# A two-layer graph network kernel: the edge phase cut into three parts, with one softmax over all edges and V and the receiver rows kept in DRAM

## The reference

```python
# layer 0: attention over the edges that end in a node, 8 heads of 32
qkv = x @ W_qkv.T + b_qkv
att = einsum('mhd,mhd->mh', Q[dst], K[src]) / sqrt(32)
e = exp(att - segment_max(att, dst)[dst])
attention = e / segment_sum(e, dst)[dst]
x = layernorm(x + segment_sum(attention * V[src], dst) @ W_ff.T + b_ff)
# layer 1: messages from the type of the sender, filtered by the edge
W = (edge_attr @ W_dist + b_dist) * cut(edge_weight)
agg = segment_sum(embed_table[node_type][src] * W, dst)
x = layernorm(x + concat([x, agg]) @ W_comb + b_comb)
```

## Time and profile before

| | before |
|---|---|
| three runs | 1411.08, 1412.26, 1413.56 us |
| median | 1412.26 us |
| span of the profiled execution | 1409.4 us |
| busy: PE, DVE, ACT, POOL | 85%, 85%, 63%, 76% |
| mean granted clock of PE | 0.972 |
| moved by DMA | 160.55 MB, 114 GB/s over the span |

### The profile page before, as it was taken

One profiled execution on the slowest core, in us unless ns is written; L12 is line 12 of the kernel. 1 busy time (PEld: TensorE's weight loads), 2 busy tenths in 40 slices (PEclk: granted clock), 3 DMA queues, 4 the chain that ended last, 5 costly groups with the idle time before them and its releaser, 6 DMA issues.

```text
span 1409.4 us, 30737 instructions
## 1 busy us (share of the span) xinstructions
PE 1197.9 (85%) x7469; PEld 1051.0 (75%) x7469; DVE 1193.5 (85%) x3044; ACT 891.5 (63%) x2560; POOL 1064.4 (76%) x1141
## 2 busy tenths in 40 slices
PE   2999999999999958888888888888888888888882
PEld 1788888888888857777777777777778777877872
DVE  3899999999999968888888888888888888888882
ACT  1788898988889954555555555555555555555541
POOL 1787878788888845877777777777877777777763
PEclk9999999999999989999999999999999999999996
DMA  5666666666666431111222221222222222222200
GB/s 165 231 228 216 229 215 228 216 225 220 228 219 227 174 118 42 52 55 56 58 59 60 61 61 58 61 61 62 62 62 62 62 62 58 62 62 62 61 29 27
DMA packets 76848, 160.55 MB, mean 114 GB/s; under 512 B 27159, under 2 KB 42514, under 8 KB 76758
## 3 DMA queue, kind: packets, MB, share of 16 engines
q1 hardware_dynamic: 59574, 124.18, 26.8%
q0 software_dynamic: 17248, 36.08, 8.5%
HBM read 98.65 MB, written 67.45 MB: 118 GB/s over the span
## 4 chain that ended last, share of the span: by engine, by line
POOL 39%; issue 34%; DVE 14%; ACT 4%; POOLq 3%; DMA 2%; PE 2%; SPq 1%; DVEq 1%; ACTq 0%
POOL zin L605 16%; POOL xd L659 6%; POOL xs L658 6%; POOL ub L667 3%; DVE den L1427 2%; DVE est L1335 2%; DVE t L1330 2%; DVE resc L1419 2%; DVE xs_lo L1325 2%; POOL ty_idx L612 2%; DVE xd_lo L1322 2%; POOL tyf L622 1%; ACT raw L1081 1%; POOL idx_b L648 1%; POOL ty L616 1%
## 5 line engine op out<-in xcount | busy, mean ns | idle before, releaser
L773 PE MATMUL ps<-w_mix,zT 128*128 128x256 f32 x1564 | 363.0, 385 | 19.6 <-ACT zT L957 18.4
L773 PEld LDWEIGHTS ps<-w_mix,zT 128*128 128x128 f32 x1564 | 290.4, 191 | 72.8 <-ACT zT L957 30.7
L605 POOL TENSOR_TENSOR zin<-xin,bff_row 128x1024 f32<-128x1024 f32 x98 | 231.9, 2367 | 2.2
L1266 DVE SCALAR_TENSOR_TENSOR yn<-ps,r,bc 128x256 f32<-128x256 f32 x391 | 162.2, 478 | 17.4 <-issue 12.2
L973 ACT ACTIVATE junk<-yn 128x256 f32<-128x256 f32 x391 | 156.9, 402 | 8.6 <-DVE yn L1266 8.4
L616 POOL DMA_INDIRECT ty<-in_node_type_dram,ty_idx x98 | 97.7, 997 | 84.3 <-DMA ty<-in_node_type_dram,ty_idx 50.4
L658 POOL DMA_INDIRECT xs<-in_x_dram,idx_b x98 | 116.7, 1191 | 52.9 <-issue 52.9
L1038 ACT ACTIVATE rdx<-rd 128x512 f32<-128x512 f32 x49 | 30.9, 631 | 197.2 <-DVE rd L1351 197.2
L699 POOL DMA_INDIRECT out_dram<-oe,idx_b x98 | 104.5, 1066 | 66.9 <-POOL idx_b L691 45.8
L1235 DVE BATCH_NORM_STATS2 stat<-zin 128x6 f32<-128x256 f32 x391 | 136.2, 407 | 4.6 <-POOL zin L605 4.6
L807 PE MATMUL ps<-xs_hi,w_hi 128*128 128x256 f32 x392 | 118.8, 303 | 11.1 <-DVE ye L1365 7.9
(11 more groups left out here) (173 smaller groups left out, 3675.7 us busy)
## 6 DMA issues: line engine op xcount, KB each, us to landing
xin<-in_x_dram SPq DMA_DIRECT2D x97, 512.0 KB, 3.7
out_dram<-on SPq DMA_DIRECT2D x97, 512.0 KB, 2.9
tybc<-type_rows SPq DMA_DIRECT2D x49, 128.0 KB, 3.4
dwin<-dst_o SPq DMA_DIRECT2D x47, 128.5 KB, 3.2
attr_o<-in_edge_attr_dram SPq DMA_DIRECT2D x1, 3125.0 KB, 13.5
at<-attr_o SPq DMA_DIRECT2D x48, 64.0 KB, 3.0
ty<-in_node_type_dram,ty_idx POOLq DMA_INDIRECT x98, 4.1
xs<-in_x_dram,idx_b POOLq DMA_INDIRECT x98, 3.4
```

Source lines behind the costliest of these rows:

```text
L605: pool.tensor_tensor(z, xx, bb, ALU.add).then_inc(n_z, 1)
L773: last = mm(ps[0:np_, 4 + 2 * (q % 2) + j // 2, (j % 2) * D:(j % 2 + 1) * D], zT[:, q % 2, k, j * P:j * P + np_], w_mix[:, k, :], start=k ...
L1266: last = dve.scalar_tensor_tensor(out=yn[0:np_, q, j * D:(j + 1) * D], in0=ps[0:np_, 4 + 2 * (q % 2) + j // 2, (j % 2) * D:(j % 2 + 1) * D ...
```

## The change

The edge phase becomes three parts, written out for all 49 blocks (no loops).

1. For every block: gathers, transposes, parts, Q, K and V. Q and K now have the edges in the partitions; their bias is added by a product of ones with the bias row. DVE multiplies them and a `tensor_reduce` over 32 channels gives the scores `att`. V and the transposed receiver rows are stored in DRAM (`v_o`, `xd_o`, 256 KB each a block).
2. The scores are transposed to 14 chunks x 8 heads = 112 partitions of 896 edges. Maximum, exponential, sum and division are done at once on [112, 896] tiles: scans inside a chunk in both directions, and short scans on one row for what crosses from chunk to chunk. The result, e / sum, goes to DRAM (`a_o`).
3. For every block SP loads back the receiver rows, V, the flags of equal receivers and the attention weights, broadcast over each head's 32 channels by four transfers. POOL multiplies weight and V, DVE scans the sums, and the rest follows as before (the roots now on ACT and DVE, the bias of the aggregate in the product, its copy on ACT).

The removed code is the old `edge` of every engine (the functions above). The core of what is added:

```diff
+        def keep(b):
+            par = b % 2
+            sp.wait_ge(e_xdc, b + 1)
+            sp.dma_start(xd_o[b], flat(xdT[:, par])).then_inc(e_xdo[par], 16)
+            if b:
+                sp.wait_ge(e_v, 2 * b)
+                sp.dma_start(v_o[b - 1], flat(vT[:, 1 - par])).then_inc(e_vo[1 - par], 16)
...
+        def static_loads(n):
+            par, h = n % 2, n // 2
+            after(sp, e_hot, n - 1)
+            sp.dma_start(tybc[:, par, :], type_blocks[n:n + 1, :].to_broadcast([P, EB])).then_inc(e_tb[par], 16)
+            after(sp, e_atc, 3 * (n - 1))
...
+                sp.dma_start(at[:, par, :, :], attr_blocks[n]).then_inc(e_at[par], 16)
+            after(sp, e_z, 2 * (n - 1))
+            sp.dma_start(flat(xd2[:, par]), xd_o[n]).then_inc(l_x[par], 16)
+            after(sp, e_ev, n - 1)
+            sp.dma_start(flat(v2[:, par]), v_o[n]).then_inc(l_ev[par], 16)
+            after(sp, e_agg, 2 * (n - 1))
+            sp.dma_start(sbc[:, par, :], row(same_o, EB * n, EB * (n + 1)).to_broadcast([P, EB])).then_inc(l_s[par], 16)
+
+        def attention_load(n):
+            par = n % 2
+            after(sp, e_ev, n - 1)
+            for q in range(HPC):
+                sp.dma_start(abc[q * HD:(q + 1) * HD, par],
+                             a_o[q:H8:HPC, EB * n:EB * (n + 1)].rearrange("(a c) n -> a c n", a=1).to_broadcast([HD, DC, EB])).then_inc(l_ev[par], 16)
...
+        for n in range(2):
+            static_loads(n)
+        sp.wait_ge(c_step, step["attention"])
+        sp.dma_start(a_o.rearrange("h (t j) -> t h j", t=NCH), a_c[:]).then_inc(c_out, 16)
+        sp.wait_ge(c_out, 16)
+        for n in range(2):
+            attention_load(n)
+        for n in range(2, B):
+            static_loads(n)
+            attention_load(n)
```

```diff
+        def weigh(n):
+            par, h = n % 2, n // 2
+            pool.wait_ge(l_ev[par], 80 * (h + 1))
+            after(pool, e_num, 2 * (n - 1))
+            pool.tensor_tensor(ev[:, par], abc[:, par], v2[:, par], ALU.mult).then_inc(e_ev, 1)
...
+        for i in range(-1, B + 4):
+            if within(i - 4):
+                scatter(i - 4)
+            if within(i + 1):
+                weigh(i + 1)
+            if within(i - 1):
+                low_parts(i - 1)
```

PE, part 1 and the order of part 3:

```diff
+        for b in range(B):
+            q_product(b)
+            if within(b + 1):
+                columns(b + 1)
+            k_product(b)
+            v_product(b)
...
+        for i in range(-1, B + 2):
+            if within(i - 1):
+                ff(i - 1)
+            if within(i - 2):
+                z_rows(i - 2)
+                mix(i - 2)
+                aggregate(i - 2)
+            if within(i + 1):
+                filters(i + 1)
```

DVE, the scores, a piece of the softmax, and part 3:

```diff
+            dve.tensor_tensor(prod[:, par], ps[:, 3 + 3 * par, :], flat(qr[:, par]), ALU.mult).then_inc(e_prod, 1)
...
+                dve.tensor_reduce(by_chunk[:, r, g:g + 2, :], heads, AX.X, ALU.add).then_inc(e_att, 1)
...
+        dve.tensor_tensor_scan(out=run_c[:], data0=neg_a[:], data1=scores_c, initial=-FAR, op0=ALU.add, op1=ALU.max).then_inc(c_step, 1)
+        dve.wait_ge(c_step, step["running_maximum"])
+        dve.tensor_tensor_scan(out=seg_c[:, ::-1], data0=neg_b[:, ::-1], data1=run_c[:, ::-1], initial=-FAR, op0=ALU.add, op1=ALU.max).then_inc(c_step, 1)
...
+        dve.reciprocal(run_c[:], a_c[:]).then_inc(c_step, 1)
...
+        for i in range(-2, B + 3):
+            if within(i):
+                sums(i)
+            if within(i - 1):
+                edge_z(i - 1)
+            if within(i - 3):
+                edge_rstd2(i - 3)
+            if within(i):
+                messages(i)
+            if within(i - 2):
+                edge_stats(i - 2)
+            if within(i + 2):
+                onehot(i + 2)
+            if within(i - 2):
+                edge_y(i - 2)
```

More of the change, by code:

```diff
@@ L176, in build @@
     on = sb("on", [P, SLOTS, ROWS * D])
[L179 to L206, removed]
@@ L223, in build @@
+    turn.close()
+    xs, xd = (sb(n, [P, 2, 2, D]) for n in ("xs", "xd"))
+    xs_hi, xs_lo, xd_hi, xd_lo = (sb(n, [P, 2, 2, EB], F32R) for n in ("xs_hi", "xs_lo", "xd_hi", "xd_lo"))
+    xdT, vT, qr = (sb(n, [P, 2, 2, EB]) for n in ("xdT", "vT", "qr"))
+    prod = sb("prod", [P, 2, 2 * D])
+    rest_e2 = sb("rest_e2", [P, 3 * D])
     s_w = sem("weights_landed")
@@ new lines, in z_rows, with mix @@
+        def z_rows(n):
+            par = n % 2
+            pe.wait_ge(e_z, 2 * (n + 1))
+            after(pe, e_st, n)
+            for t in range(2):
+                for c in range(DC):
+                    last = pe.transpose(bank(1)[:, t, c * P:(c + 1) * P], zeT[:, par, c, t * P:(t + 1) * P], ident[:])
+            last.then_inc(e_zp, 1)
+        def mix(n):
+            pe.wait_ge(e_zh, n + 1)
+            pe.wait_ge(e_zl, n + 1)
+            after(pe, e_y, 2 * n)
+            edge_rows(bank(2), z_hi, z_lo, lambda k: mix_hi[:, k, :], lambda k: mix_lo[:, k, :], None).then_inc(e_mixp, 1)
@@ new lines, in _, with sums @@
+        dve.wait_ge(c_step, step["reciprocal"])
+        dve.tensor_tensor(a_c[:], ex_c[:], run_c[:], ALU.mult).then_inc(c_step, 1)
+        def sums(n):
+            par = n % 2
+            dve.wait_ge(l_s[par], 16 * (n // 2 + 1))
+            dve.wait_ge(e_ev, n + 1)
+            after(dve, e_num, 2 * n)
+            after(dve, e_ffp, n - 1)
+            for c in range(2):
+                dve.tensor_tensor_scan(out=num[:, par, c, :], data0=sbc[:, par, :], data1=ev[:, par, c, :],
+                                       initial=num[:, 1 - par, c, EB - 1:EB] if n else 0.0, op0=ALU.mult, op1=ALU.add).then_inc(e_num, 1)
@@ new lines, in edge_y @@
+        def edge_y(n):
+            par = n % 2
+            dve.wait_ge(e_s1, n + 1)
+            after(dve, e_y, 2 * n)
+            dve.reciprocal(er1[:], esd1[:]).then_inc(e_r1, 1)
+            dve.wait_ge(e_r1, n + 1)
+            dve.wait_ge(e_mixp, n + 1)
+            dve.wait_ge(e_t2, n + 1)
+            after(dve, e_oe, 2 * (n - 1))
+            for t in range(2):
+                dve.scalar_tensor_tensor(out=ye[:, par, t, :], in0=bank(2)[:, t, :], scalar=er1[:, t:t + 1], in1=t2[:, t, :],
+                                         op0=ALU.mult, op1=ALU.add).then_inc(e_y, 1)
```

999 lines of the change are left out of this document (511 added, 488 removed).

## The result

| | us (lowest to highest of four runs) | ratio to before, 95% interval |
|---|---|---|
| before, beside it | 1411.85 | |
| changed, first set of runs | 1431.95 (1429.29 to 1434.18) | 1.0144 (1.0129 to 1.0159) |
| changed, again, with the experiments | 1462.22 (1457.07 to 1464.65) | 1.0348 (1.0318 to 1.0378) |

The changed kernel is slower, as forecast: 1.4% in the first runs, 3.5% in a second set on a chip where the kernel before takes the same 1412. The forecast, 1452, lies between the two. The profiled execution of the first set has a span of 1430.5 us.

What follows compares the result with a forecast made beforehand. No engine was full; a chain through the engines bound the kernel. First z at 849 us, 47 turns of 12.1 (569) to 1418 and a tail of 31 gave a span of 1449, so 1452 us; range 1365 to 1505.

Steps and rivals of the forecast that it cites:

- The loop by which ev waits for a whole load in each turn: Part 3: SP waits for z(n-2), then seven issues, landing, ev, sums and z in series; 12.1 us a turn, chance 0.50.
- P: Part 3, rival theory from the trace after, not in the prediction: PE and ACT wait in a ring, about 11.8 us.
- The transfers: Part 3, the loads of a turn: six steps between SP's seven issues 2.8 us, landing 3.3.
- ev 1.28, two hops 0.15: Part 3: POOL's ev takes 1.28 us; the hops between engines, 0.15, include that from ev to DVE's sums.
- 3.7 for the two sum scans: Part 3: DVE's two sum scans, 1.3 to 1.39 us alone, take 3.7 beside POOL's agg_lo and z_lo.
- rival (a): Part 3: same loop, scans hardly slowed (2.4) or loads landing sooner (2.8); turn 10.4, 1372 to 1400 us; chance 0.22.
- a second loop of 9.6 at full and 11.8 at half clock over two turns: Part 3: z_lo to mix, aggregate, filter, ff, z, loads, ev; 19.2 us over two turns, 23.5 with half clock.
- Rival (b): Part 3: the load is hidden and the busiest engine sets a turn of 8.2 us: 1268 us; chance 0.06.
- Rival (c): Part 3: PE idles, stays at the lower clock, its work 13.5 us a turn: 1518 us; chance 0.17 with (d).
- (d): Part 1: its turn isn't near 6 us; at 7.2 the kernel takes 1516 us; chance 0.17 together with Rival (c).
- gaps at waits: Part 1, PE: gaps where it waits lift a turn from 5.5 to 5.9 us.
- disputed term: Part 2, softmax: the reciprocal of 896 elements, taken as 5 us, between 1.1 and 14; 7.5 by the Trainium skill.

Runs made afterwards that it cites:

- e1: Changed kernel with SP issuing xd2 last, so that its wait for z stands behind the block's other loads: 1380.58 us.
- e6: Changed kernel with 16 products into an unused PSUM bank ahead of PE's wait for atT, to hold the clock up: 1458.07 us.
- e2: Changed kernel with ACT's copy of the transposed attributes (atT) put ahead of its copies of agg_hi and z_hi in part 3: 1448.19 us.
- f4: Changed kernel with atT copied first, types and attributes loaded one block earlier, and POOL's two low-part subtractions ahead of ev: 1344.25 us.
- e3: Changed kernel with the type row and attributes loaded one block earlier, ahead of the loads that wait for z: 1449.54 us.
- f2: Changed kernel with xd2 loaded last and types and attributes loaded one block earlier, ACT's order of copies kept: 1400.99 us.
- c1: Changed kernel with three edits: xd2 loaded last, types and attributes one block earlier, atT copied first on ACT: 1261.18 us.
- f1: Changed kernel with xd2 loaded last and atT copied first, the type row left behind the attention: 1289.06 us.
- c0: The changed kernel run again without any edit, beside the experiments: 1462.22 us.
- e5: Changed kernel with two more 64-byte transfers issued by SP behind v2, ahead of the same row and the attention quarters: 1467.21 us.

## Why the prediction was right, point by point

**Direction and mechanism: right, and shown.** The loop by which ev waits for a whole load in each turn sets the turn: moving one wait (e1) takes 82 us, raising the clock (e6) 4, shortening P (e2) 14, of which 6 lie ahead of part 3; and 1.49 us less for the sums (f4) come back in the turn in full.

**The turn, 12.1 against 11.85, is right through two errors that cancel.** The transfers were right: 2.8 and 3.3 forecast, 6.1, measured 6.20; ev and z were right. The step "ev 1.28, two hops 0.15" missed what is queued ahead of the sums on DVE: the hop is 1.12, since onehot waits for a type row that SP issues behind the attention. The prediction listed what stands behind SP's wait only as far as ev needs it. The step "3.7 for the two sum scans" was 1.36 too long: measured 2.34, below the 3 to 4 that the prediction named as its sign, with a group mean of 1209 ns over 96 and single ones up to 1748. Its mechanism holds: where the sums start at ev's end (e3) they take 3.27, and with POOL out of the way (f4) 1.43. The sum was too long because the missed wait let half of the slowing pass. So rival (a) had the right scans (2.4), and the forecast has the right turn by luck, as far as these two terms go.

**The loops below.** The prediction had a second loop of 9.6 at full and 11.8 at half clock over two turns. There is a ring of about these sizes (f2: 9.4 and 11.1), but it runs otherwise, through ACT's order of copies, over one turn; that step was right in size and wrong in kind.

**Rival (b)**, the busiest engine alone, 8.2: it appears once all the waits are moved, as 7.67 (c1). Of the loads summed in the prediction PE's 7.8 was too high (329.60 us in 350 is 7.2 a turn of c1) and DVE's 6.9 too low (326.91, 7.2 too), since its scans and onehot are slowed. f1's 8.24 is next to 8.2 by chance: the type row's loop sets it. **Rival (c)**, the lower clock: the clock was 0.85 in part 3, and e6 shows that it didn't matter. **(d)**, part 1 above 5.9: 5.6 in the first set and 6.1 in c0, far from its 7.2 in both.

**Part 1.** First Q product at 509.63 (forecast 508). PE full, full clock, products 0.12 apart as in the earlier trace rows, turns of 5.56 in the median; last V product's end at 785.2, forecast 799. The term at fault was the 0.4 of "gaps at waits": there are none in the first set. In c0 there are.

**Part 2.** 51.3 us from the last V product to the end of z(0), forecast 50. The softmax itself, from the table operations at 785.15 to the end of a_c at 818.37, is 33.2, forecast 33. Its disputed term:

```profile
787.11 2.01 DVE L1449 TENSOR_TENSOR_SCAN run_c<-neg_a,ps 112x896 f32<-112x896 f32 x1
...
811.50 5.75 DVE L1501 RECIPROCAL run_c<-a_c 112x896 f32<-112x896 f32 x1
```

The reciprocal took 5.75, between my 5 and the estimate of 7.5 worked out from the Trainium skill's "VectorE: DVE Perf Modes", section "Walkthrough: the 8-slice pipeline in each mode"; the scans took 2.01 and not 2.3.

**The tail** was 37.2 from z(47) (1393.35 to 1430.5), forecast 31; the last three blocks run at a mean clock of 0.72. **The sum:** z(0) 12.5 early, 47 turns 12.1 less, the tail 6.2 more, and 1.5 in place of 2.9 outside the span make 19.8, the difference between 1451.8 and 1431.95.

## What to carry to other kernels

When a queue waits for a result, list everything issued behind that wait, and for each item who waits for it and what stands behind *that* engine's wait: the loop here held seven issues, and a type row nobody had in mind held up the sums. Where several loops lie close together, no edit alone shows its worth (14, 13 and 82 us alone, 201 together), so try them in pairs before dropping one. The order of work on POOL is part of DVE's speed: put POOL's SBUF arithmetic where no DVE instruction of the path that reads SBUF alone, such as the scans and onehot here, runs beside it.

## What the runs showed of the hardware

- Two scans of 256 elements take 1.39 to 1.43 us, 3.27 to 3.3 beside two 128x512 subtractions on POOL (2.9 us together), of which the second lengthens from 1.27 to 1.65.
- A comparison of 256 elements a lane (onehot, one tile read) takes 0.35 us alone and 1.26 in the mean beside a POOL subtraction (f1); ye, which reads one of its two inputs from PSUM, 0.48 in both cases.
- A transfer of 128 KB whose source goes 4 heads, 32 copies, 256 elements lands as if on a quarter of the DMA engines: a share of 0.24, landing 5.39 us in place of 2.71.
- A reciprocal of 896 elements takes 5.75 us.
- The same kernel ran 30 us apart in two sets while the kernel before ran within 2 us, nearly all of it ahead of part 3. In the one block compared, PE's releases reached POOL 1.4 and ACT 1.8 us later. The cause is open.
- An issue of 64 bytes takes 0.27 us of the queue and lengthens a burst by 0.25 (e5), next to the 0.45 of a quarter of the attention (64 KB).
